# The stage behind graph attention: its products and sums all on VectorE, and the first exponentials among ScalarE's fills

## The reference

```
Wh = (x @ W.T).reshape(N, H, C)
e = e_left[src] + e_right[dst];  e = leaky_relu(e, 0.2)       # edges and self loops
e_max = segment_max(e, dst)
e_exp = exp(e - e_max[dst])
alpha = e_exp / (segment_sum(e_exp, dst) + 1e-16)
out = segment_sum(Wh[src] * alpha[:, :, None], dst)
x = _layernorm(x + out)
```

## Time and profile before

| | us |
|---|---|
| median of three runs (lowest, highest) | 4839.53 (4834.4, 4844.5) |
| the profiled execution: time | 4835.31 |
| its span, first to last instruction | 4833.5 |
| busy in the span: DVE | 3287.3 (68%) |
| busy: POOL | 3261.1 (67%) |
| busy: PE | 2608.6 (54%) |
| busy: ACT | 1038.7 (21%) |

### The profile page before, as it was taken

One profiled execution on the slowest core, in us unless ns is written; L12 is line 12 of the kernel. 1 busy time (PEld: TensorE's weight loads), 2 busy tenths in 40 slices (PEclk: granted clock), 3 DMA queues, 4 the chain that ended last, 5 costly groups with the idle time before them and its releaser, 6 DMA issues. The chain is left out here.

```text
span 4833.5 us, 43726 instructions
## 1 busy us (share of the span) xinstructions
PE 2608.6 (54%) x11566; PEld 1932.2 (40%) x11566; DVE 3287.3 (68%) x9285; ACT 1038.7 (21%) x2639; POOL 3261.1 (67%) x3361
## 2 busy tenths in 40 slices
PE   6221065555755556744460000278776977688875
PEld 5110043333533334411140000266665866577664
DVE  6798565555665566888867888766665666566665
ACT  3333334444344443000021111220001000010002
POOL 3777747776477763777747777457774777757773
PEclk8555575555755558766675555589888988899887
DMA  2656636665366651655626766246663666546663
GB/s 88 225 192 221 212 115 209 209 209 200 130 209 209 209 174 59 206 200 202 201 73 196 222 220 219 79 139 215 218 215 124 209 216 217 192 148 214 217 213 122
DMA packets 266264, 887.61 MB, mean 184 GB/s; under 512 B 68539, under 2 KB 104744, under 8 KB 221992
## 3 DMA queue, kind: packets, MB, share of 16 engines
q0 software_dynamic: 157728, 428.39, 30.5%
q1 hardware_dynamic: 108296, 456.51, 24.4%
HBM read 438.85 MB, written 445.80 MB: 183 GB/s over the span
## 5 line engine op out<-in xcount | busy, mean ns | idle before, releaser
L1311 POOL DMA_INDIRECT WORK<-table,SRCI x1376 | 1324.6, 963 | 580.3 <-issue 483.6
L1311 POOL DMA_INDIRECT WORK<-table,BYSRC x1092 | 1058.6, 969 | 444.8 <-issue 414.9
L1337 PE MATMUL e_pm<-ARENA 128*128 128x256 f32 (+1 forms) x4200 | 1012.0, 403 | 0.0
L1388 DVE SCALAR_TENSOR_TENSOR WORK<-WORK,LOWE 128x256 f32<-128x256 f32 x1288 | 625.6, 486 | 460.6 <-DMA WORK<-table,BYSRC 370.6
L1337 PEld LDWEIGHTS e_pm<-ARENA 128*128 128x128 f32 (+1 forms) x4200 | 840.8, 204 | 150.8 <-issue 28.9
L1388 DVE SCALAR_TENSOR_TENSOR WORK<-WORK,NST,e_mv 128x256 f32<-128x256 f32 x1173 | 562.8, 480 | 496.8 <-issue 228.4
L1355 ACT ACTIVATE e_mv<-WORK,WE 128x256 f32<-128x256 f32 x1176 | 491.2, 463 | 832.8 <-DMA WORK<-table,SRCI 790.7
L1734 POOL DMA_INDIRECT WORK<-table_attention,SRCI x392 | 373.4, 952 | 119.4 <-issue 119.1
L898 PE MATMUL e_rb<-ARENA 98*128 98x128 bf16 x392 | 114.7, 293 | 439.9 <-ACT ARENA L914 439.9
L1405 DVE TENSOR_TENSOR ARENA<-e_pr,ARENA 128x640 f32<-128x640 f32 x420 | 314.1, 813 | 17.1 <-PE e_pr L1322 17.1
L962 PE MATMUL e_hi<-ARENA 128*128 128x392 bf16 x392 | 176.8, 451 | 233.0 <-DVE ARENA L948 232.6
(11 more groups left out here) (386 smaller groups left out, 5050.5 us busy)
## 6 DMA issues: line engine op xcount, KB each, us to landing
edge_results<-WORK SPq DMA_DIRECT2D x343, 1024.0 KB, 4.6
edge_results_attention<-WORK SPq DMA_DIRECT2D x98, 544.0 KB, 3.2
table<-ARENA SPq DMA_DIRECT2D x35, 640.0 KB, 3.2
WORK<-table,SRCI POOLq DMA_INDIRECT x1376, 3.7
WORK<-table,BYSRC POOLq DMA_INDIRECT x1092, 3.6
WORK<-table_attention,SRCI POOLq DMA_INDIRECT x392, 2.8
table_attention<-ARENA SPq DMA_DIRECT2D x5, 660.0 KB, 3.5
ARENA<-table,SRCI POOLq DMA_INDIRECT x192, 2.9
```

Of the source, the lines that this page charges most:

```text
L1311: eng.indirect_dma_start(slot(g, k), None, T, bass.IndirectOffsetOnAxis(ap=index[:, t:t + 1], axis=0)).then_inc(got[q].sem, 16)
L1337: last = eng.matmul(made_ps[:, i % 4, 0:D], hot_rows[0:n, i % 2, j, :], AGG[0:n, j, :], start=j == 0, stop=j == NT - 1)
L1388: eng.scalar_tensor_tensor(O[:, q % OB, k, :], behind, mask[:, ds(g * GT + k, 1)], here, op0, op1).then_inc(linked, 1)
```

## The change

POOL's instruction stream ends with its 25 gathers. Its product of `C` by the share and its sum into `X` are done by DVE, within `join(k)`; the semaphores `weighed` and `pooled` are gone. The order within `join` is: `YW`, `AGW` and `C` by their shares, `YW` + `AGW`, `X` + `C`, `X` + `YW`. The product of `AGW` is counted, but nothing waits for it alone. On ACT the exponentials of chunk 0 stand behind the fills of the first ten tiles instead of behind all 25; the others stay behind the fills.

```diff
                 def _(eng):
                     for t in range(NT):
                         got = gathered[t // u]
                         eng.indirect_dma_start(YW[:, t, :], None, PA, bass.IndirectOffsetOnAxis(ap=end_sum[:, t:t + 1], axis=0)).then_inc(got.sem, 16)
-                    for k in range(NT // u):
-                        eng.wait_ge(weighed, k + 1)
-                        eng.tensor_tensor(by_head(C, k), by_head(C, k), share(2, k), ALU.mult).then_inc(pooled, 1)
-                        eng.wait_ge(pooled, 2 * k + 1)
-                        eng.tensor_tensor(X[:, chunk(k), :], X[:, chunk(k), :], C[:, chunk(k), 0:D], ALU.add).then_inc(pooled, 1)
...
-                    for t in range(NT):
+
+                    def fill(t):
                         eng.wait_ge(crossed, t + 1)
                         eng.activation(AGW[:, t, 0:TW], across[:, t % 3, 0:TW], ACT.Copy).then_inc(filled, 1)
                         eng.activation(AGW[:, t, TW:RW], across[:, t % 3, TW:RW], ACT.Identity, bias=ALONE[:, 0, t:t + 1]).then_inc(filled, 1)
-                    for k in range(NT // u):
+
+                    def exponentials(k):
                         eng.wait_ge(scored, k + 1)
                         eng.activation(e_[:, :, chunk(k)], z_[:, :, chunk(k)], ACT.Exp).then_inc(expd, 1)
+
+                    for t in range(2 * u):
+                        fill(t)
+                    exponentials(0)
+                    for t in range(2 * u, NT):
+                        fill(t)
+                    for k in range(1, NT // u):
+                        exponentials(k)
...
-                        eng.sem_inc(weighed, 1)
 
                     def join(k):
                         T = chunk(k)
                         c.inc(eng.tensor_tensor(by_head(YW, k), by_head(YW, k), share(0, k), ALU.mult))
-                        c.link(eng.tensor_tensor(by_head(AGW, k), by_head(AGW, k), share(1, k), ALU.mult))
-                        c.link(eng.tensor_tensor(YW[:, T, 0:D], YW[:, T, 0:D], AGW[:, T, 0:D], ALU.add))
-                        eng.wait_ge(pooled, 2 * k + 2)
+                        c.inc(eng.tensor_tensor(by_head(AGW, k), by_head(AGW, k), share(1, k), ALU.mult))
+                        c.link(eng.tensor_tensor(by_head(C, k), by_head(C, k), share(2, k), ALU.mult))
+                        c.inc(eng.tensor_tensor(YW[:, T, 0:D], YW[:, T, 0:D], AGW[:, T, 0:D], ALU.add))
+                        c.link(eng.tensor_tensor(X[:, T, :], X[:, T, :], C[:, T, 0:D], ALU.add))
                         c.link(eng.tensor_tensor(X[:, T, :], X[:, T, :], YW[:, T, 0:D], ALU.add))
```

More of the change, by code:

```diff
@@ L1874, in attention_nodes @@
                 names = ("chain", "expd", "scored", "turned", "back", "maxed", "weights", "weighted", "selected", "crossed", "filled",
-                         "weighed", "pooled", "spread", "rooted_rows", "scaled_rows", "staged", "xturned", "xt", "made", "moved", "moved_last",
+                         "spread", "rooted_rows", "scaled_rows", "staged", "xturned", "xt", "made", "moved", "moved_last",
                          "stored")
                 (chain, expd, scored, turned, back, maxed, weights, weighted, selected, crossed, filled,
-                 weighed, pooled, spread, rooted_rows, scaled_rows, staged, xturned, xt, made, moved, moved_last,
+                 spread, rooted_rows, scaled_rows, staged, xturned, xt, made, moved, moved_last,
                  stored) = (st.sem(n) for n in names)
```

## The result

The changed kernel took 4820.1 us (median of six runs, 4814.26 to 4820.91), the kernel before, measured beside it, 4837.7 (six runs). The ratio is 0.9961, with a 95% interval of 0.995 to 0.9973: 18.9 us less by the ratio, 17.6 by the two medians. The forecast was 21.9 us less and 4815.5 us, with a range of 4807 to 4830. The profiled execution took 4816.71 us against 4835.31, 18.6 less, and all but 0.1 of that lies ahead of the end of the stage: the first instruction of the next stage has moved from 3190.30 to 3171.77, by 18.5 us.

The account below looks back on a forecast made before the run. No engine bounds the whole; the changed stage follows DVE's chain. 36.0 us gone less 14.1 added gives 21.9 less: 4813.4 from the profiled execution, 4817.6 from the median, middle 4815.5 us, range 4807 to 4830.

Parts of the forecast that it names:

- (a): ACT's fills: the first exponential behind the tenth fill instead of all 25 lets shares(0) start 7.6 us earlier.
- ahead of the selections, and what is late next is DVE itself: Start of shares(0): exponential ends near 3070.4, selections at 3072.62, so shares(0) starts at about 3072.7, 7.6 us earlier.
- (b): Chunk 0's join: DVE's sum X + YW no longer waits for POOL's product behind its 25th gather; 10.0 us gone.
- (c): DVE lines L2034, L2035 and L2052 return to clean durations without POOL's arithmetic beside them; 18.4 us gone.
- Added: Five joins on DVE: one product and one sum more each, +2.82 us per join, +14.1 us in all.
- The end: Behind join(4): a fixed tail, 20.7 us from the last square root to the next stage's first instruction.
- The rival in which gathers stand still during the joins: Joins 0 and 1: POOL's gathers halt, scores(4) waits 7.1 us; gain only 14.8 us, 4822.6 us; chance 0.06.
- the forecast end near 3096: POOL's last gather, slowed beside joins 0 and 1 by 5 us, ends near 3096 instead of 3091.35.
- The prediction's reading of the rule: Gathers beside two-input DVE operations: the Trainium skill's port rule was read as not slowing gathers at all.
- The slower rival: Joins 0 and 1: gathers hold DVE, 2.67 us per operation, 32 us; net +10.1, 4847.5 us; chance 0.04.
- The third, a gain given back behind the stage: Later passes: one runs 12 or more us longer, leaving 4827 to 4840 us, no change; chance 0.09.

Follow-up runs that it names:

- the changed kernel again: The changed kernel measured once more with no edit: 4808.74 us, ratio 0.9953 to the kernel before.
- The run on scratch: Changed kernel, with POOL again making one product and one sum per chunk, on scratch nobody reads or waits for: 4836.66 us, ratio 1.0013.
- the run with fills: Changed kernel, with POOL making two write-only fills with zero per chunk, no input from SBUF: 4813.8 us in its one run, stage 112.3.
- the other part: Changed kernel with the exponentials back behind all 25 fills, DVE making all products and sums: ratio 0.9981, stage 118.7 us.

## Why the prediction came out as it did

The time lies in the range, and the mechanisms of the three terms are the forecast ones; the sum was 3 us too large. By its own terms, in the profile after, with the stage's total of 18.7 us:

- (a) ACT's exponential: forecast 7.6, measured 3.4. From the first scan to shares(0) it was 22.68 us before and is 19.32. The mechanism was right: the first exponential is among the fills (3074.71) and DVE doesn't wait for it. The size was off, because the sum took the end of the selections from a profile in which PE's clock had risen at the fourth tile. The step that was off is "ahead of the selections, and what is late next is DVE itself": next was PE. Of the 4.2 us missing, 1.4 came by way of the fifth fill, for which scores(0) waits, and 2.8 by way of the ring. With three slow tiles (the changed kernel again) the term was 7.8.
- (b) The wait on POOL: forecast 10.0, all of it gone; no join has an idle ahead of its last sum.
- (c) DVE beside POOL's arithmetic: forecast 18.4, all of it gone; products at 1.48 to 1.49, the factors at 0.16 to 0.17 five times. The run on scratch shows that POOL's arithmetic does it without any wait or shared data, the run with fills that its writes don't; what is left is POOL's reads.
- Not counted: the `sem_inc` on `weighed` was an instruction of its own between shares and join. From the first operation of shares to join it was 2.04 us in chunk 0 and 1.68 in chunk 1; now it is 1.56 and 1.57. That is 0.5 us once and 0.1 three times (chunks 1, 3 and 4); in chunk 2 the wait for ACT's root stands there, and the stretch is 0.1 longer (1.88 us, 1.80 before). In all 0.7 us of gain. The run with fills, which has the instruction again, shows 2.04 and 1.68 again. Why it costs more in chunk 0 is open.
- Added: 14.1 forecast; chunk 2 from its first product to the next shares is 11.35 us against 8.54, 2.81 per join.
- The end: 20.6 against 20.8.

3.4 + 10.0 + 18.4 + 0.7 - 14.1 + 0.2 = 18.6, against 18.7 measured. In the changed kernel's second profile, with three slow tiles, it is 7.8 + 10.0 + 18.4 + 0.7 - 14.1 - 1.2 (its longer end) = 21.6, as measured. So 21.9 comes out there to 0.3 us partly by luck: a gain of 0.7 and a loss of 1.2, neither of them in the sum, nearly cancel. The forecast of the time itself, 4815.5, is a weaker test: the same program took 4820.1 us in one measurement and 4808.74 in the other, where the kernel before had moved too, from 4837.7 to 4830.86.

The rival in which gathers stand still during the joins did not come: the gathers of the changed kernel beside join(0) took 1.97 us for the first and 1.09 to 1.22 for the next five, 2.0 us more than six quiet ones (forecast 2.5 per join). The last ended at 3091.98, ahead of join(1) at 3093.59, so the second join met none, and the forecast end near 3096 was 4 us too late.

```profile
3078.99 1.97 POOL L1907 DMA_INDIRECT ARENA<-edge_results_attention,end_sum  x1 [0.30 <-issue]
3081.27 1.10 POOL L1907 DMA_INDIRECT ARENA<-edge_results_attention,end_sum  x1 [0.30 <-issue]
```

Yet the joins do hold the gathers, one at a time. The gather at 3078.99 ended 2.31 us behind the start of the first product (3078.65), the one at 3081.27 ended 2.31 behind the start of the second (3080.06), and so on through the six operations. The same holds in all thirteen profiles, 2.29 to 2.32 us for 75 pairs, whenever the gather began: the first of a row takes 1.11 to 2.15 us, the more the earlier it starts beside the first product. The prediction's reading of the rule, by which the gathers would not be slowed at all, is not borne out. So beside such a row one gather passes per DVE operation, every 1.4 to 1.5 us instead of every 1.25. It costs little only because these operations are hardly longer than a gather. With longer ones it should cost more, which no run here tried.

The slower rival fell as well: DVE's six operations beside the gathers took 1.48 or 1.49 each. The third, a gain given back behind the stage, didn't come either: 18.5 of the 18.6 us stand at the end of the stage. What the prediction lacked was a term for PE's clock. It looked at ACT's fills as ended by ACT, when they follow PE tile by tile, and a look at the windows ahead of 3072 would have shown a clock of 0.50 and 0.75 that might as well have stayed low.

## What to carry to other kernels

Work handed to an idle engine isn't free when that engine and the busy one both read SBUF: here POOL's product and sum cost DVE 4.6 us in each of four chunks, and doing them itself costs it 2.8. Two waits that lie over each other must be priced together: the early exponential alone gave 0.9 us; on top of the other part it gave 4.7 to 7.7 (stages of 114.0 and 111.0 against 118.7). A stretch in which PE has just begun to work should be priced at both clocks before a sum is built on its end.

## What was not expected of the hardware

- Between 3 and 17 of 25 products ran at the low clock in nine profiles of programs with the same PE work, and 3 and 12 in two profiles of one program, which moved the start of join(0) by 4.4 us. The Trainium skill (TensorE: Matmul & The Clock Gate, "Part 1: The HAM clock gate") says that the number of slow products at the start of a kernel varies between runs; the profiles agree, for a start inside a kernel too.
- A DVE operation of 5 or 40 columns with two inputs in SBUF, 0.17 to 0.20 us alone, takes 2.0 to 2.9 us when a POOL operation with such reads has begun ahead of it. The profile books this as busy time of DVE.
- Gathers beside DVE operations of 128x1280 with two inputs take 1.09 to 1.22 us instead of 0.95, and the first one 1.11 to 2.15: each ends 2.3 us behind the start of one such operation, which is 0.8 behind its end. What exactly of a gather waits is open.
